# Softmax sums in an attention and FP8 block: from an inverted, spread and multiplied form to sums moved to all rows of a head and inverted there

## The reference

```
x = x + attention(layernorm(x), Wq, Wk, Wv, Wo, W_down_kv, W_up_k, W_up_v)
x = x + ffn(layernorm(x), kernel, input_scale, kernel_scale, bias)

def attention(x, ...):
    q = x @ Wq ; k = x @ Wk ; v = x @ Wv
    latent_kv = (k + v) @ W_down_kv
    k_rec = latent_kv @ W_up_k ; v_rec = latent_kv @ W_up_v
    scores = einsum('bhqd,bhkd->bhqk', heads(q), heads(k_rec)) * scale   # clipped
    scores = scores * exp(-0.0001 * |i - j|)                             # clipped
    attn = softmax(scores, axis=-1)
    return heads_back(einsum('bhqk,bhkd->bhqd', attn, heads(v_rec))) @ Wo

def ffn(x, ...):
    x_q = (x / s_in).astype(float8_e4m3fn) ; k_q = (kernel / s_k).astype(float8_e4m3fn)
    return bf16(x_q @ k_q * (s_in * s_k)) + bias
```

## Time and profile before

| | |
|---|---|
| median of 3 runs | 513.15 us (513.13 to 513.18) |
| profiled execution | 513.14 us |
| its span | 511.3 us |
| ScalarE busy | 486.7 us (95%) |
| TensorE busy | 478.2 us (94%) |
| VectorE busy | 268.5 us (53%) |
| GpSimd busy | 218.5 us (43%) |
| granted clock of TensorE | 0.99 of full speed |

### The profile page before, as it was taken

The page is one execution under the profiler, slowest core; times in us unless marked ns, Lnnn a source line. Parts: engine busy times, 40 slices in busy tenths (PEclk is TensorE's granted clock), DMA queues, the critical chain, the costliest instruction groups (busy, mean ns, idle before and its releaser), DMA issues.

```text
span 511.3 us, 9473 instructions
## 1 busy us (share of the span) xinstructions
PE 478.2 (94%) x3456; PEld 113.3 (22%) x3456; DVE 268.5 (53%) x639; ACT 486.7 (95%) x541; POOL 218.5 (43%) x285
## 2 busy tenths in 40 slices
PE   7899999999999999999999999999999999899991
PEld 3312221132122212222121221223121212122220
DVE  6514554555554564646644554544644555445536
ACT  3789999999999999999999999999999999999983
POOL 0889509883720249873450229957101031002110
PEclk9999999999999999999999999999999999999996
DMA  6589979877543326647834223568744222220000
GB/s 185 182 252 230 333 168 222 319 211 229 164 97 87 73 56 213 219 129 236 261 78 98 67 68 120 173 217 252 247 96 128 67 68 69 55 56 2 1 22 24
DMA packets 56755, 73.79 MB, mean 144 GB/s; under 512 B 6976, under 2 KB 32256, under 8 KB 56704
## 3 DMA queue, kind: packets, MB, share of 16 engines
q1 hardware_dynamic: 55616, 72.72, 49.4%
q10 hardware_dynamic: 1088, 0.41, 0.3%
HBM read 35.40 MB, written 35.65 MB: 139 GB/s over the span
## 4 chain that ended last, share of the span: by engine, by line
PE 43%; ACT 39%; issue 12%; DVE 4%; DMA 1%; ACTq 0%; DVEq 0%
ACT probs L803 38%; PE ps L1019 22%; PE ps L1003 12%; PE ps L999 2%; PE ps L913 1%; PE ps L908 1%; DVE ps L1269 1%; PE ps L880 1%; DVE pv_out L1282 1%; PE ps L876 1%; DMA wuv_s<-L_attn_W_up_v 1%; DVE mv L1316 0%; PE ps L933 0%; PE ps L870 0%; PE ps L885 0%
## 5 line engine op out<-in xcount | busy, mean ns | idle before, releaser
L803 ACT ACTIVATE probs<-ps 128x1024 f32<-128x1024 f32 x512 | 473.4, 1101 | 5.8 <-DVE ps L1269 2.6
L1019 PE MATMUL ps<-probs,V 128*9 128x512 f32 x2048 | 267.8, 595 | 0.4 <-DVE pv_out L1282 0.4
L1269 DVE TENSOR_TENSOR ps<-ps,consts 128x256 f32<-128x256 f32 (+1 forms) x256 | 140.6, 564 | 157.2 <-PE ps L1003 150.7
L1003 PE MATMUL ps<-Qs,Ks 64*128 64x512 bf16 x992 | 171.8, 384 | 13.9 <-ACT probs L803 11.8
L1003 PEld LDWEIGHTS ps<-Qs,Ks 64*128 64x128 bf16 x992 | 44.6, 93 | 283.6 <-ACT probs L803 271.8
L1282 DVE COPY pv_out<-ps 105x512 f32<-105x512 f32 x28 | 19.4, 691 | 58.0 <-PE ps L1019 58.0
L605 POOL TENSOR_SCALAR rs<-mv 128x4 f32<-128x4 f32 (+1 forms) x10 | 2.3, 228 | 99.2 <-DVEq L1456 98.5
L1019 PEld LDWEIGHTS ps<-probs,V 128*9 128x9 f32 x2048 | 30.5, 88 | 62.2 <-issue 54.3
L688 POOL TENSOR_TENSOR xs<-xs,magic 128x512 f32<-128x512 f32 x7 | 8.9, 1273 | 56.5 <-DVE magic L1335 56.5
L701 POOL TENSOR_TENSOR yb<-yb,bias_s 128x512 bf16<-128x512 bf16 x7 | 8.1, 1155 | 49.9 <-DVE yb L1407 49.5
L641 POOL TENSOR_TENSOR parts<-sq,parts 128x1024 bf16<-128x1024 f32 (+1 forms) x16 | 28.7, 1791 | 1.3
(11 more groups left out here) (152 smaller groups left out, 285.0 us busy)
## 6 DMA issues: line engine op xcount, KB each, us to landing
Qs<-qp_dram SPq DMA_DIRECT2D x58, 256.0 KB, 4.6
qp_dram<-parts SPq DMA_DIRECT2D x14, 768.0 KB, 6.3
Ks<-kp_dram SPq DMA_DIRECT2D x28, 256.0 KB, 3.9
kp_dram<-parts SPq DMA_DIRECT2D x12, 384.0 KB, 4.4
kp_dram<-parts SPq DMA_DIRECT2D x6, 768.0 KB, 5.1
Ks<-kp_dram SPq DMA_DIRECT2D x34, 128.0 KB, 2.8
qp_dram<-parts SPq DMA_DIRECT2D x7, 512.0 KB, 8.1
X<-L_attn_x SPq DMA_DIRECT2D x9, 256.0 KB, 2.9
```

Source lines behind the costliest of these rows:

```text
L803: nc.scalar.activation(probs[:, quad % RING, 2 * jp:2 * jp + 2, :].rearrange("p j n -> p (j n)"), ps_all[:, bank * CH:(bank + 2) * CH], AC ...
L1003: last = nc.tensor.matmul(bank, Ks[half, g, jp, key_cols(v, kc)], Qs[half, g, jp, qh, v, :], start=True, stop=True)
L1019: last = nc.tensor.matmul(pv[32 * j:32 * j + VW, :], V[:, unit // 2 * NB + kc, HG * j + g, :], probs[:, quad % RING, j, :], start=i == 0, ...
L1269: nc.vector.tensor_tensor(own, own, factors, ALU.mult).then_inc(fixed, 1)
```

## The change

`den` becomes as large as the output: the transfer of a head's sums reads its one row of 512 sums eight times and fills all 8 rows of the head (16 KB in place of 2 KB; the number of transfers and of pieces stays). The inversion then runs over 128x512 elements in place, in three steps: 192 columns in quad 7, 192 in quad 11, 128 in quad 13. The product `o_raw` by `den` into `OT` runs in two steps: 384 columns in quad 12 and 128 in quad 13, after the third inversion; both operands are in SBUF. The side job "sp", the mask product into `wide`, the constants `same_head` and `place` and the two semaphores between VectorE and TensorE go; `wide`, still used by the last unit, takes over a part of `den`.

```diff
 for _u in range(1, UNITS):
     JOBS += [(_u * UNIT_QUADS + _q, _k, _u - 1) for _q, _k in (
-        (10, "sp"), (14, "proj"), (TAIL_ROWS[_u], "xqT"), (TAIL_PRODUCTS[_u], "y"))]
+        (14, "proj"), (TAIL_ROWS[_u], "xqT"), (TAIL_PRODUCTS[_u], "y"))]
...
-        den = sb("den", [P, 2, CH // HD])
-        rec = sb("rec", [P, CH // HD])
-        wide = sb("wide", [P, CH])
+        den = sb("den", [P, 2, CH])
+        rec = sb("rec", [P, 4 * HG])
+        wide = den[:, UNITS % 2, :]
...
                     sp.dma_start(den[HD * h:HD * h + HD, unit % 2, :],
-                                 pv_out[32 * j + HD:32 * j + HD + 1, group % 2, :].rearrange("p (c t) -> p c t", c=HD)
-                                 ).then_inc(moved[group % 2], 16)
+                                 pv_out[32 * j + HD:32 * j + HD + 1, group % 2, :].rearrange("p (o n) -> p o n", o=1)
+                                 .broadcast_to([1, HD, CH])).then_inc(moved[group % 2], 16)
...
-            def invert_sums(unit):
-                for i in range(2):
-                    dve.wait_ge(moved[i], 16 * 2 * HG * 2 * (unit + 1))
-                step(nc.vector.reciprocal(rec[:, :], den[:, unit % 2, :]))
...
+            sum_cols = (slice(0, 192), slice(192, 384), slice(384, CH))
+            def invert_sums(unit, i):
+                if i == 0:
+                    for parity in range(2):
+                        dve.wait_ge(moved[parity], 16 * 2 * HG * 2 * (unit + 1))
+                own = den[:, unit % 2, sum_cols[i]]
+                step(nc.vector.reciprocal(own, own))
+            def divide_by_sums(unit, cols):
                 settle()
...
+                return nc.vector.tensor_tensor(OT[:, unit % 2, cols], o_raw[:, unit % 2, cols], den[:, unit % 2, cols], ALU.mult)
...
                 if at == 7:
-                    invert_sums(unit)
-                    widen_sums(unit)
+                    invert_sums(unit, 0)
+                elif at == 11:
+                    invert_sums(unit, 1)
+                elif at == 12:
+                    step(divide_by_sums(unit, slice(0, sum_cols[1].stop)))
+                elif at == 13:
+                    invert_sums(unit, 2)
+                    divide_by_sums(unit, sum_cols[2]).then_inc(ot_ready, 1)
```

More of the change, by code:

```diff
@@ L904, in sum_oks @@
                 nc.tensor.matmul(bank[0:1, 0:1], oks[:, 0:1], ones[:, :], start=True, stop=True).then_inc(flag_ps, 1)
-            def spread_sums(unit, bank):
-                pe.wait_ge(spread, unit + 1)
-                nc.tensor.matmul(bank, same_head, wide[:, :], start=True, stop=True).then_inc(spread_ps, 1)
             def project_o(unit, bank):
@@ L956, in job @@
                     sum_oks(work)
-                elif kind == "sp":
-                    spread_sums(i, work)
                 elif kind == "turn":
@@ L1498, in finish @@
                 residual(unit)
-                for at in range(13, 28):
+                for at in range(14, 28):
                     tail(unit, at, 0)
```

30 lines of the change are left out of this document (6 added, 24 removed).

## The result

The changed kernel takes 516.7 us, the median of 4 runs (515.06 to 517.07), against 513.15 us before: a ratio of 1.0063, with a 95% interval of 1.005 to 1.0075. It is slower by 3.5 us. Six later runs on another chip had a median of 518.5 us (517.17 to 522.03), against 513.29 us for the kernel before beside them: 1.0116 (1.0094 to 1.0138). The profiled execution took 516.74 us with a span of 514.9 us, 3.6 us longer than that of before, and that difference is what the traces can account for.

A forecast was written before the change was run, and what follows sets the result against it. ScalarE's back-to-back exponentials were taken as the bound. From 513.14 us, 1.1 was subtracted for removing "sp" and 3.3 added for divisions waiting on GpSimd, transfers counted zero: 515.3 us, range 513.3 to 517.4.

The forecast's parts named there:

- the signs that it named: Quads 9 to 17: 14.67 to 14.7 us in even units, 15.5 to 16.1 in odd; "proj" waits three times.
- The bound and its ruler: ScalarE's exponentials run back to back, 0.917 us each; a longer `copy_pv` distance means scores came late.
- Gain of 1.1 us for "sp": Quads 9 to 17: without "sp", 0.7 us from six units, 0.3 from unit 7, 0.1 for smaller waits.
- VectorE's new work hidden: Quads 7, 11, 12 and 13: 4.47 us a unit replacing 1.91 costs nothing; unit 7 late by 0 to 0.2 us.
- A proj late by L costs about L: Quads 14 and 15: lateness costs L - 0.22 us, plus up to 0.2 us from TensorE's backlog.
- GpSimd, 3.3 us: Quads 12 and 13: divisions wait for GpSimd, losing 1.4, 0.9 and 1.0 us in units 1, 3 and 5.
- I count zero: Transfers of `den`, 2 KB instead of 256 bytes per piece, cost nothing; a 0.3 us wait is paid by shorter quad 7.
- The rivals: Caught twice, 517.2 us (0.14); only the gain, 512.0 (0.11); some escape or nothing, 512.9 to 514.1 or 513.1 (0.15).
- Caught twice: Unit 3's division of 128 is also held by GpSimd, "proj" late by 2.8 us: 517.2 us; chance 0.14.
- escaped: Some of units 1, 3, 5 avoid GpSimd: 512.9 to 514.1 us (0.15 including no effect); all three: 512.0 us (0.11).
- The rules: Inversion at eight cycles, estimated 8.3 ns an element, sum 2 us higher; on the shared port, the instruction issued first blocks the other fully.

The follow-up runs named there:

- experiment 1, no_product: Kernel before with only TensorE's side-job product taken out, VectorE unchanged; 512.07 us, ratio 0.9979.
- experiment 7: Changed kernel with each of the three inversions cut to 16 columns, most sums not inverted; 514.59 us, ratio 1.0043.
- Experiment 4: Changed kernel with GpSimd's late queries in units 1, 3 and 5 waiting until the division is done; 513.73 us, ratio 1.0017.
- experiment 3: Changed kernel with the old 2 KB transfers, the other 448 columns of `den` set to ones; 515.22 us, ratio 1.0056.
- wide_transfers, experiment 2: Kernel before with only the sums' transfers widened to 16 KB, still inverting 64 columns; 516.88 us, ratio 1.0051.
- experiment 10: Changed kernel, first inversion in quad 8, GpSimd's late queries and unit 1's late keys after divisions, inverse deviations before squares; 516.92 us, ratio 1.0077.
- experiment 9: Changed kernel, first inversion in quad 8, GpSimd's late queries and unit 1's late keys held until after the divisions; 517.73 us, ratio 1.0083.
- experiment 8: The changed kernel itself, unaltered, run again on another chip beside the kernel before; 518.51 us, ratio 1.0116.

## Why the prediction was right, and where it was not

The forecast was 515.3 us, slower; measured were 516.7, inside the range of 513.3 to 517.4, and slower. Against the profiled execution of 516.74 the sum is 1.4 us too low. By the distances the account is: -1.10 for the product, +1.29, +1.18 and +0.86 for GpSimd in units 3, 5 and 1, +1.42 for the transfers, together +3.65; the prediction had -1.1 + 0.9 + 1.0 + 1.4 + 0. Of the signs that it named, the even units came as it said (14.66 and 14.67) and units 3 and 5 too; unit 1 lay above (16.95 for 15.5 to 16.1), "proj" waited four times and not three, and the division of 128 was held in one unit and not in three. Step by step:

- **The bound and its ruler** (ScalarE back to back, distance of `copy_pv`): right. The differences of that distance alone add up to the change in span.
- **Gain of 1.1 us for "sp"**: right, 1.10 us by experiment 1, 0.14 or 0.15 in each even unit and 0.25 in unit 7 where 0.3 stood.
- **VectorE's new work hidden**: right. The inversions took 1.34 and 0.94 us and the divisions alone 0.55 and 0.29, as worked out from the earlier trace rows; experiment 7 shows them to be free in even units and to cost 0.17 us in unit 7.
- **"A proj late by L costs about L"**: right to 0.12 us. 1.41, 1.29 and 0.97 us late cost 1.29, 1.18 and 0.86.
- **GpSimd, 3.3 us**: right in mechanism, wrong in its parts, and right in sum (3.33 us) by luck. Experiment 4 takes it away in units 3 and 5. They lost 1.29 and 1.18 us where 0.9 and 1.0 stood. Unit 1 lost 0.86 where 1.4 stood, and that it lost anything hung on the transfers, which the prediction had put at nothing: they delayed the unit by 1.42 us and so put the division of 128 behind the late queries. In experiment 3, without that delay, it started 0.12 us before them and the unit lost nothing. The prediction had it 0.25 us behind them. In unit 5 the division of 384 was caught, with the inversion still to come, and not that of 128. The step that failed is the start of GpSimd's late queries, which I took from one execution: 6.13 us after the copy of quad 9 in unit 5, by the kernel before. In the changed kernel it came 4.90 us after it, and in six other variants 4.5 to 5.2, in wide_transfers and no_product too, where no division moved. In unit 3 it is 4.71 in the kernel before and 4.7 to 5.3 elsewhere. So the row of unit 5 in the earlier trace rows was the odd one among eight profiles, and the two units are alike. In unit 3 the 0.3 us by which the late queries started later than in the earlier trace rows (5.01 us after the copy for 4.71) are most of what its loss was too small by.
- **"I count zero" for the transfers**: wrong, and the largest miss. They cost 1.42 us in unit 1, and 2.28 with the meeting that they brought about. I had read the one wait of 0.3 us in quad 7 of unit 1 and set the shorter work of that quad against it. What I left out is that the DMA engines are busy throughout there, and that this was to be seen. DMA of the kernel before from 80 to 95 us, and of the changed kernel (second row of each: share of 16 engines' time):

```profile
DMA  9999999999999999999999657999999999999998
...
q1 hardware_dynamic: 3241, 4.05, 105.1%
```

```profile
DMA  9999999999999999999999999998999999999999
...
q1 hardware_dynamic: 3189, 3.82, 109.0%
```

Into that stretch eight times as many bytes of sums were put, and their last landed late: the inversion started at 94.05 in the changed kernel, at 95.27 with wide transfers alone, at 92.24 before and at 91.92, waiting for nothing, with the narrow ones. In all other units quad 7 waits for nothing in either kernel. More than half of the lateness arose well ahead of that stretch, where SyncE issues the transfers one after the other. Timeline of SyncE, changed kernel and kernel before:

```profile
62.66 1.61 SPq L488 DMA_DIRECT2D o_raw<-pv_out  x1
```

```profile
62.56 0.63 SPq L490 DMA_DIRECT2D o_raw<-pv_out  x1
```

This one issue took 1.0 us longer, all behind it came later by as much, and the last transfer that the inversion needs was issued at 88.64 in place of 87.57 (at 87.67 with the narrow transfers, at 88.99 with the wide ones alone). From there to the inversion it took 5.41 us in place of 4.67. So of the 1.81 us by which the inversion started later, 1.07 lay ahead of the issue and 0.74 behind it. What held the issue up is not shown; with narrow transfers it took 0.63 us.

- **The rivals.** "Caught twice" in unit 3 did not happen in the changed kernel: after the division of 384 GpSimd's next instruction was the L636 that copies, and the division of 128 slipped past the start of the next. Something like it happened in experiment 7, by L636 and for some 0.5 us, where the inversion was shorter, not longer. The time of 517.2 us that the prediction gave it came out near the measured one for another reason, the transfers. All three units met GpSimd; none escaped.
- **The rules.** By the repeat count of 8 in the Trainium skill, VectorE: DVE Perf Modes, First, the fixed hardware budget, read as eight cycles, the inversion of 192 elements would have taken an estimated 1.6 us; it took 1.34, as the rows of before said. By the Trainium skill, SBUF — State Buffer, Who interferes with whom, the GpSimd instruction that comes second is blocked until the other is done. L636 started at 224.11 with 0.35 us of the division of 384 left and took 1.25 us, 1.04 being its length alone: 0.21 longer, so the trace shows it held, but for less than what was left.

The changed kernel on a second chip took 1.8 us more than on the first. Both are slower than before, and the second is above the range that I gave. The profiled execution there was only 0.4 us longer than the one here, of which 0.37 lie ahead of the first copy; its wait for the transfers cost 0.4 us more and its meetings with GpSimd 0.3 less. What made the other five longer, and whether it is TensorE's clock, stays open.

## What to carry to other kernels

A transfer that grows in bytes has a price where the DMA engines are busy throughout, and the stretch to look at is the one with the most traffic, not the mean; a wait of 0.3 us that occurs once marks the place. Look also at the engine that issues, where one late issue delays all behind it. An operand that moves from PSUM to SBUF makes a VectorE product a neighbour of GpSimd: look for what GpSimd does there, and hold it back with a semaphore if it has time, but follow all that GpSimd does afterwards to the next one who waits for it. And a loss read in one profiled execution belongs to that execution's time, not to the median.

## What the runs showed of the hardware

- Half clock, 0.50 (1.2 GHz), followed on TensorE's pauses of 1.45 and 0.53 us (experiment 2, for 3.4 us), and of 2.48, 0.52 and 0.53 us (experiment 10, for 3.4 us), and in experiment 9 it came within a pause of 2.96 us and lasted 6.8 us. The clock stayed at 1.00 (2.4 GHz) with pauses of 0.59, 0.53 and 0.53 us in the changed kernel, of 1.00, 0.52 and 0.53 in experiment 8, and of 1.14, 0.53 and 0.53 in experiment 4. In these profiles a wait of VectorE of 2.2 us for the transfers cost 1.4 us, one of 2.7 us cost 2.0, and one of 3.0 us, with the half clock behind it, 3.6.
- VectorE's `tensor_scalar` with one tile in SBUF as input (and two scalars per partition), f32 to bf16, was held up by GpSimd as a product of two SBUF inputs is: four took 4.43 us for 1.11, ending 0.58 us after it. The Trainium skill, SBUF — State Buffer, Who interferes with whom, counts `tensor_scalar` among the operations that can take the pair of ports shared with GpSimd; this trace agrees.
- A division of n elements that was held ends a fixed time after GpSimd's instruction: 0.42 us for 384 elements (units 3 and 5 of the changed kernel), 0.15 for 128 (unit 1), 0.54 for the 512 of the earlier trace rows. That is 1.05 to 1.2 ns for each of its elements, as if all of them were done after GpSimd's end.
- When a transfer that releases an engine lands differs between executions and variants by about a microsecond: GpSimd's late keys began at 99.53 and 98.61 us in two profiles of one kernel, taken on two chips. A collision that hangs on it is there in one run and not in the next.
